# Scans over four overlapping quarters, score parts summed by TensorE, and the division on ScalarE, in a four-layer graph attention kernel

## The reference

```
0: Wh = h W;  e_ij = leaky_0.2(s_i + s_j);  x += elu(softmax(e) Wh)                                         (4 heads)
1: e_ij = leaky_0.01(s1_i + s2_j);  x += h W + softmax(e) h                                               (1 head)
2: x' = h W + b;  e_ij = leaky_0.2(s_i + s_j);  x += softmax(e) x'                                         (4 heads)
3: q, k, v = h Wq + bq, ...;  x += softmax(q k / 8 + mask) v                                               (4 heads)
```

## Time and profile before

| | |
|---|---|
| time, median of 3 runs | 2071.25 us (2067.58 to 2077.36) |
| the profiled execution | 2069.63 us, span 2067.8 us |
| instructions | 25285 |
| busy, DVE | 1667.1 us (81%) |
| busy, PE / weight loads | 1321.1 us (64%) / 953.6 us (46%) |
| busy, POOL | 1159.4 us (56%) |
| busy, ACT | 797.0 us (39%) |
| mean granted TensorE clock | 0.841 |

### The profile page before, as it was taken

How to read it: one execution, slowest core, us unless ns; L and a number is a source line. 1 busy time by engine, 2 the same in 40 slices (tenths; PEclk the granted TensorE clock), 3 DMA queues, 4 the chain that set the end, 5 groups by cost and what they waited for, 6 DMA issues and landing times. The chain is left out here.

```text
span 2067.8 us, 25285 instructions
## 1 busy us (share of the span) xinstructions
PE 1321.1 (64%) x7813; PEld 953.6 (46%) x7813; DVE 1667.1 (81%) x4333; ACT 797.0 (39%) x1634; POOL 1159.4 (56%) x1172
## 2 busy tenths in 40 slices
PE   3556332666766626777778257788786477777775
PEld 2434221554554414555555144455553355555553
DVE  2878897899999746787777279989995599999996
ACT  5777353576676501222223013223322223333332
POOL 0000057777775057777773377777750677676660
PEclk9999999887787757887778569989999689888887
DMA  9999124454553034444442345555541677676660
GB/s 353 388 386 344 20 67 128 123 134 130 132 131 99 16 102 115 124 126 124 122 126 76 82 112 136 154 160 157 148 127 57 217 235 228 213 222 212 214 218 12
DMA packets 162363, 324.07 MB, mean 157 GB/s; under 512 B 31274, under 2 KB 79280, under 8 KB 162224
## 3 DMA queue, kind: packets, MB, share of 16 engines
q0 software_dynamic: 64512, 191.91, 34.4%
q1 hardware_dynamic: 80016, 109.35, 15.5%
q10 hardware_dynamic: 17696, 21.12, 2.9%
HBM read 290.39 MB, written 31.90 MB: 156 GB/s over the span
## 5 line engine op out<-in xcount | busy, mean ns | idle before, releaser
L792 POOL DMA_INDIRECT s_gb<-s_tab,s_ji x1152 | 1155.1, 1003 | 599.9 <-issue 343.3
L1864 PE MATMUL ps<-s_gb,s_S 128*128 128x264 f32 (+1 forms) x2304 | 640.3, 439 | 41.0 <-DVE s_gb L1561 40.8
L1864 PEld LDWEIGHTS ps<-s_gb,s_S 128*128 128x128 f32 x2304 | 497.9, 222 | 138.3 <-DVE s_gb L1561 43.6
L1561 DVE TENSOR_TENSOR s_gb<-s_gb,ps 128x768 f32<-128x768 f32 x384 | 349.7, 944 | 4.6 <-ACT ps L995 4.5
L1788 PE MATMUL ps<-s_wx,s_hT 128*128 128x264 f32 (+2 forms) x512 | 242.5, 613 | 158.7 <-ACT s_tb L941 73.2
L995 ACT ACTIVATE ps<-s_sc 128x72 f32<-128x72 f32 (+3 forms) x68 | 15.0, 220 | 608.7 <-DVE s_sc L1508 608.7
L1788 PEld LDWEIGHTS ps<-s_wx,s_hT 128*128 128x128 f32 x512 | 119.2, 257 | 224.1 <-ACT s_tb L941 81.2
L978 ACT ACTIVATE s_S<-s_count,s_ji 128x128 f32<-128x128 f32 x576 | 174.8, 387 | 90.5 <-PE ps L1864 75.2
L1828 PE MATMUL ps<-s_qs,s_ST 128*128 128x256 bf16 x864 | 145.7, 338 | 58.5 <-DVE s_tmp L1477 41.2
L1840 PE MATMUL ps<-s_ident,s_sc 128*16 128x128 f32 (+3 forms) x408 | 61.8, 293 | 146.3 <-DVE s_sc L1455 146.3
L1828 PEld LDWEIGHTS ps<-s_qs,s_ST 128*128 128x128 fp8e4 x864 | 100.9, 121 | 100.8 <-DVE s_tmp L1477 49.3
(11 more groups left out here) (199 smaller groups left out, 1852.6 us busy)
## 6 DMA issues: line engine op xcount, KB each, us to landing
s_adj<-in_adj_dram SPq DMA_DIRECT2D x32, 2048.0 KB, 17.4
s_gb<-s_tab,s_ji POOLq DMA_INDIRECT x1152, 3.0
s_mine<-s_tab SPq DMA_DIRECT2D x128, 128.0 KB, 3.0
s_tab<-s_tb ACTq DMA_DIRECT2D x32, 256.0 KB
s_tab<-s_tb ACTq DMA_DIRECT2D x31, 260.0 KB
s_qs<-s_q SPq DMA_DIRECT2D x32, 192.0 KB, 4.3
s_q<-s_qs SPq DMA_DIRECT2D x15, 384.0 KB, 2.9
s_xs<-in_x_dram SPq DMA_DIRECT2D x8, 512.0 KB, 16.0
```

The source lines that it names most:

```text
L792: e.indirect_dma_start(gb[:, 0, k, 0:L.row], None, self.tab_d[L.n], bass.IndirectOffsetOnAxis(ap=self.idx[:, t, k:k + 1], axis=0)).then_in ...
L1561: e.tensor_tensor(vv[:, k], vv[:, k], wide(p[:, k, :], 3, L.hd), ALU.mult).then_inc(self.weighed)
L1864: m = e.matmul(o, S[:, i, :], g4[:, 0, k, lo:lo + D + 2 * L.heads], start=(k == 0), stop=(k == KT - 1))
```

## The change

1. **Scans.** The edges are covered by four overlapping stretches of 4 blocks (HC = 4, HS = 4) in place of two of 6. A pair fills 32 partitions and the scans have 512 columns. Four transposes of 32 columns replace six of 16, both ways; `seg_d` is stored by four DMAs and holds four stretches. Score tiles are laid out with raw and own parts apart, 10 blocks long.
2. **Score parts.** `pe_expand` writes two views (one in layer 3), and the three bf16 parts are accumulated in PSUM by three matmuls each. The reduction L1437 goes, and `first` is added when the row's own score is read from PSUM.
3. **Division and ELU.** In layers 0, 2 and 3 DVE's `vec_finish` ends with the sum in PSUM (`summed`). ACT's new `act_scale` multiplies it per head by the reciprocal (four Copy activations) into `y`, which has now two buffers. In layer 0 it goes on with Relu(-y) and Exp of its negative. `act_exp_elu` and the early table load `act_exp_table` go. DVE's `vec_settle`, which has moved behind the shift, adds the results to x.
4. **Norms.** `vec_norm` is issued after the second of the six products of weighing.

```diff
-FW = EC + 16
+FW = EC + 136
-HC = 6
+HC = 4
+HS = 4
...
-            self.y = s2("y", [P, D])
+            self.y = s2("y", [P, 2, D])
-            self.F = s2("F", [16, HE])
-            self.d0 = s2("d0", [16, 2, HW], BF16)
-            self.sc, self.sc2 = s2("sc", [P, 2, 2 * KT * 8]), s2("sc2", [P, 96])
+            self.F = s2("F", [32, HE])
+            self.d0 = s2("d0", [32, 2, HW], BF16)
+            self.sc, self.sc2 = s2("sc", [P, 2, 2, (KT + 1) * 8]), s2("sc2", [P, HC * HS * 8])
...
-        for half in range(2):
-            self.sp_dma(e, self.seg_d[:, 2 * half:2 * half + 2, :], self.segb[:, 3 * P * half:3 * P * half + HW], self.seg_in)
-        e.wait_ge(self.seg_in, 32)
+        for s in range(HS):
+            self.sp_dma(e, self.seg_d[:, 2 * s:2 * s + 2, :], self.segb[:, 2 * P * s:2 * P * s + HW], self.seg_in)
+        e.wait_ge(self.seg_in, 16 * HS)
...
+    def act_scale(self, e, L, t):
+        g, j, H = T * L.n + t, t % 2, L.heads
+        before = T * max(L.n - 1, 0) + t - 1
+        y, ov = self.y[:, j, :], self.out_bank(L, t)[1]
+        e.wait_ge(self.summed, T * max(L.n - 1, 0) + t + 1)
+        if before > 0:
+            e.wait_ge(self.x_new, before)
+        for h in range(H):
+            m = e.activation(y[:, L.hd * h:L.hd * h + L.hd], ov[:, L.hd * h:L.hd * h + L.hd], ACT.Copy,
+                             scale=self.rc[:, j, h:h + 1])
+        m.then_inc(self.evac)
+        if L.n == 0:
+            em = self.em[:, j, :]
+            e.wait_ge(self.evac, g + 1)
+            e.activation(em, y, ACT.Relu, scale=-1.0).then_inc(self.ex_in)
+            e.wait_ge(self.ex_in, t + 1)
+            e.activation(em, em, ACT.Exp, scale=-1.0).then_inc(self.ex_out)
...
+        if scale:
+            self.act_scale(e, L, 2 * n)
         if L.n == 0:
-            self.act_exp_elu(e, 2 * n)
             self.act_onehot(e, L, 2 * n + 2)
         if n:
             self.act_turned(e, l, n - 1)
-        if L.n == 0:
-            self.act_exp_elu(e, 2 * n + 1)
+        if scale:
+            self.act_scale(e, L, 2 * n + 1)
         self.act_exp(e, L, n + 1)
...
             self.act_onehot(e, L, 2 * n + 2)
+            self.act_scale(e, L, 2 * n)
+            self.act_scale(e, L, 2 * n + 1)
+            self.act_onehot(e, L, 2 * n + 3)
...
-        e.tensor_reduce(sc[:, :, :, 2 * H - w:2 * H].rearrange("p k t h -> p (k t) h"),
-                        sx.rearrange("p (c s h) -> p c h s", c=KT * c, s=3), AX, ALU.add).then_inc(self.v)
+        e.tensor_tensor(split(z), self_, first, ALU.add).then_inc(self.v)
...
-        for s in range(2):
-            m = e.tensor_tensor(twice[:, :, s], raw[:, 3 * s:3 * s + HC], z[:, 3 * s:3 * s + HC], ALU.max)
+        for a in (0, 2):
+            r, q = (x[:, a:a + 8].rearrange("p (s k) m -> p s k m", s=HS) for x in (raw, z))
+            m = e.tensor_tensor(twice[:, :, a:a + 2], r, q, ALU.max)
...
-        e.tensor_tensor(by_head(y[:]), by_head(ov), wide(rc, 2, L.hd), ALU.mult).then_inc(self.evac)
+        e.tensor_tensor(ov, ov, mine, ALU.add).then_inc(self.summed)
...
+        if L.n == 0:
+            e.wait_ge(self.ex_out, t + 1)
+            e.scalar_tensor_tensor(x, y, 0.0, x, ALU.max, ALU.add).then_inc(self.v)
+            e.wait_ge(self.v, vs.up())
+            e.scalar_tensor_tensor(x, self.em[:, t % 2, :], -1.0, x, ALU.add, ALU.add).then_inc(self.x_new)
+        else:
+            e.wait_ge(self.evac, g + 1)
+            e.tensor_tensor(x, x, y, ALU.add).then_inc(self.x_new)
...
-        self.vec_done(e, L, t[0])
+        self.vec_finish(e, L, t[0])
         if n < 16:
             self.vec_shift(e, L, n + 1)
-            if L.n == 0:
-                self.vec_mutual(e, n + 1)
+        self.vec_settle(e, L, t[0])
+        self.vec_stats(e, t[0])
+        if L.n == 0 and n < 16:
+            self.vec_mutual(e, n + 1)
...
             for k in range(KT):
-                o = 3 * w * (k * c + t)
-                m = e.matmul(sx[:, o:o + 3 * w].rearrange("p (s h) -> p s h", s=3),
-                             self.ST[:, tiles[t], P * k:P * k + P], self.si3[:, tiles[t], :, 0:w], start=True, stop=True)
+                for i, view in enumerate(views):
+                    for s in range(3):
+                        m = e.matmul(view[:, k, j, :], self.ST[:, t, P * k:P * k + P],
+                                     self.si3[:, t, s, H * i:H * i + H], start=(s == 0), stop=(s == 2))
```

## The result

2092.2 us (median of 4 runs, 2091.5 to 2094.0) beside 2071.7 of the kernel before: ratio 1.0098, 95% interval 1.0073 to 1.0123. I had forecast 2086, slower. The profiled execution took 2092.7, its span 2090.9.

A forecast was written before the change was run, and what follows sets the result against it. Bounds taken: layer 1 gathers, layer 2 nearly so, layer 0 PE's chain and DVE arriving together, layer 3 PE nearly as late as DVE. 16+0+12-16+4 = +16 on 2069.6, the runs' median 1.6 above: 2086 us, range 2046 to 2108.

The forecast's parts named there:

- Sign and size: Whole kernel: slower, 2086 us, because PE's and ACT's additions stand in the chain DVE waits for.
- the chain over PE and ACT: ACT, projection, expansion, additions: what is put on it delays DVE's finish of the first tile; layer 0 ACT +1.45, expansion +2.45.
- DVE is the bound: Rival, whole kernel: the added chain is hidden; layer 0 -25, layer 2 -4, layer 3 -35, total 2007 us; 8%.
- Durations: Instruction costs taken: scan 1.19 us, expansion matmul 28 ns, four copies 1.05 us, DVE's busy total down some 140 us.
- The clock: Layer 0, PE's first additions: more work ahead should start them at the higher clock, -0.85 to 0 us from 5.10.
- The rival that let the clock pay: Longer bursts keep PE at 2.4 GHz: layer 3 -27, layer 0 +3, layer 2 +4, total 2051 us; 17%.
- the step that I worked out, 22.85: Layer 0's period after the change, 22.85 us a pair: +1.1 a pair, 15 pairs, +16 us (-25 to +30).
- The step that I started from, 21.72: Layer 0's period before the change, read from one step: additions done at 10.5 us, DVE there at 10.7.
- Layer 2: +1.8 us in the step read, -0.3 where gathers hold it; mean +0.8 a pair, +12 us (-4 to +27).
- Layer 3: Scans and some of the reduction count, division's saving mostly lost: -1.1 us a pair, -16 us (-35 to 0).
- Layer 1: Bound by gathers: DVE's saving and PE's extra work disappear in 4.4 us of waiting a pair; 0.
- Ends: Ends of layers: scans saved, expansion and uncovered scale added, +1 a layer three times, segment stores +1; sum +4 us.

The follow-up runs named there:

- e6: e3 with 90 idle 4-column matmuls added ahead of each expansion in layer 0 alone; 2044.9 us.
- e3: The change with only the scans over four stretches (the quarters) and the norm's earlier place; score parts and division as in the kernel before; 2007.7 us.
- e8: e3 with score parts accumulated in PSUM in layer 3 alone; 2000.3 us, 3.1% under the kernel before.
- e1: The change with score expansion and reduction put back as before, division still on ACT; 1.4% of before's time above e3.
- e2: The change with division put back on DVE as before, score parts still in PSUM; 2.2% of before's time above e3.
- e7: e3 with the norm moved back behind the whole weighing; as expected (2010 us), the norm's place does nothing.
- e9: The whole change with PE's two pauses by layer 0's projections filled with 26 and 12 idle transposes in 13 steps; 2080.7 us.
- e10: e8 with PE's pauses in 13 steps of layer 0 filled with 4 and 30 idle transposes; 1990.4 us.
- e11: The change with 54 expansions of 8 columns for 108 of 4, layer 0's PE pauses filled with 26 and 14 idle transposes; 2876 us, before 2605 there.
- e12: The same kernel as e11, run again on another chip; 2862 us where the kernel before took 2556.

## Why the prediction was right, step by step

- **Sign and size:** +20 where +15 was forecast. It rests on the chain over PE and ACT, and the waits it named are there: DVE for PE's first additions 3.3 us a pair in layer 0 (39.5 in 12) and some 3.0 in layer 2 (40.1 with the second tiles' 0.3 each), DVE for ACT 1.5 ahead of settling the second tile. That the total is so near is in part luck: against the forecast the layers are off by +4, -6, +10 and -7 us, the ends by +6. The forecast's own terms also add to 2087, not 2086. The chance of 8% for "DVE is the bound" was fair of the whole change, and wrong of its first part: alone the quarters give 2007.7. That this is almost the rival's 2007 is chance, since the rival priced the whole change and had nothing at the ends.
- **Durations:** scans 1.20 and 1.21 (1.19 taken), 108 expansions 3.07 (28 ns each, as read from the earlier trace rows), four copies 0.93 (1.05), Exp's table in the first tile's chain of layer 0, DVE 142 us less (140). From DVE's arrival to the next subtraction: 8.86 (8.85).
- **The clock was taken with the wrong sign.** I gave the additions 4.25 to 5.1 us because more work would stand ahead; they took 5.66, and the clock of layer 0 went from 0.78 to 0.71. In e6, 90 short matmuls make the additions behind them 1.0 us longer. The rival that let the clock pay had 17%; that was too much. This is most of the difference between the step that I worked out, 22.85, and the 23.90 that came. The step that I started from, 21.72, was one of the shorter kind: against the mean of both kinds the additions grew from 5.48 to 5.70, and layer 0 is +1.9 a pair where +1.1 was forecast.
- **Layer 2:** the step that I worked out, +1.8, is what came in the mean, +1.7, but I averaged it down to 0.8 with steps held by the gathers; all 12 pairs were the chain's. That the mean agrees is in part luck. Six of 11 steps took 24.6, less than the 25.1 worked out; five took 26.1 to 27.4, because their first additions ran at the low clock for a part, 5.9 or 7.1 us in place of 4.25, which I had at nothing. The longer projection behind PE's pause was in my step already (3.27), though not in 6 of 11 steps before.
- **Layer 3:** -1.6 a pair in place of -1.1. The order was right: e3 has -1.17 for the quarters, e8 -0.5 more for the reduction, and the division moves it by less than 0.1 (e1 against e3, after against e2).
- **Layer 1:** 0 forecast, -0.5 measured. The DVE waits for data remained (60.9 us in 13, 52.4 in 12 before), so it is the gathers: 980 ns in place of the 1003 of the earlier trace rows, with 0.30 us between them as before. Every variant has it, e7 too; what they share is the quarters. Why, no run shows.
- **Ends:** +10 in place of +4; 4.1 of it lies between layers 0 and 1. What makes it up, no run takes apart.

## What to carry to other kernels

A busy total, even one at 92%, doesn't say which way a trade goes: here taking work off the bound engine pays when the work goes away (quarters, -3%), and loses when it is handed to engines whose chain ends right beside it (+4%). Take such a change apart before judging it; and before putting an activation of another table, or a hundred small matmuls, ahead of a long one, look at what the next engine's pause does to its clock, for here the table load's 1.28 us became 2.2 a pair, and the short matmuls' 2.4 became 3.3. And read more than one step: before, layer 0 alternated between two kinds, and the forecast rested on one of them.

## What the runs showed beside this

- A scan's time goes by its columns, not its partitions: 1.72 us for 768 in layers 0 and 1 alike, in 16 and in 4 partitions, and 1.20 for 512 in 32 and in 8 (14.38 in 12 and 15.69 in 13).
- With its pauses filled, PE's clock in e9 still fell for 6.8 us at a run of 108 matmuls of 4 columns; with 18 of 24 columns in that place (e10) it never fell. The two kernels differ in the division and in the filling too, so that the short matmuls are what lets it fall is not shown.
- On the two chips of e11 and e12, PE stops within the run of short matmuls with nothing to wait for that the profile shows; e12, PE, layer 0:

```profile
618.17 0.64 PE L1853 MATMUL ps<-s_si,s_ST 128*128 128x8 bf16 x17
619.28 0.18 PE L1853 MATMUL ps<-s_si,s_ST 128*128 128x8 bf16 x1 [0.47 <-issue]
620.67 0.18 PE L1853 MATMUL ps<-s_si,s_ST 128*128 128x8 bf16 x1 [1.20 <-issue]
```

Over the execution that is 408.9 us in 309 waits. It fits instructions that come too slowly, and a kernel with many short ones losing most by it (ratio 1.105 and 1.119 there). That is a guess: neither was tried apart, and no trace of the kernel before is from these chips.
